# Attention scratch stores: two images per first store, keys by halves of the tokens, weight loads ahead of the stores

## The reference, cut to what matters

```python
def _dilate_attention(q, k, v, head_dim, scale, ksz, dil):      # l0
    ...
    attn = jnp.einsum('bncl,bnckl->bnlk', qr, kp) * scale
    attn = jax.nn.softmax(attn, axis=-1)
    out = jnp.einsum('bnlk,bnckl->bnlc', attn, vp)
```

## Time and profile before

| What | us |
|---|---|
| median of 3 runs | 901.85 |
| profiled execution, its own time | 900.02 |
| its span, first to last instruction | 898.4 |
| TensorE matmuls busy | 668.9 |
| VectorE busy | 403.3 |
| ScalarE busy | 299.2 |
| GpSimd busy | 133.0 |
| TensorE waiting at line 705 for `k_parts` | 35.9 |

### The profile page before, as it was taken

How to read it: one execution, slowest core, us unless ns; L and a number is a source line. 1 busy time by engine, 2 the same in 40 slices (tenths; PEclk the granted TensorE clock), 3 DMA queues, 4 the chain that set the end, 5 groups by cost and what they waited for, 6 DMA issues and landing times. The chain is left out here.

```text
span 898.4 us, 12568 instructions
## 1 busy us (share of the span) xinstructions
PE 668.9 (74%) x3958; PEld 551.4 (61%) x3958; DVE 403.3 (45%) x1010; ACT 299.2 (33%) x594; POOL 133.0 (15%) x185
## 2 busy tenths in 40 slices
PE   5848855998977999519869980299990498698397
PEld 2536634696774999516557770299990267576286
DVE  3647845216255333054648844032311546586501
ACT  2323423223223454113225431044440143245222
POOL 5311110003000000242340003300005306100000
PEclk9988987698988999858879985599996588799689
DMA  3783200533014364113685304347622138751153
GB/s 106 162 222 80 77 19 32 129 101 112 1 39 119 104 178 121 41 53 78 170 248 114 67 7 145 117 109 184 176 67 66 37 80 227 197 124 32 40 131 93
DMA packets 87826, 94.42 MB, mean 105 GB/s; under 512 B 16689, under 2 KB 75972, under 8 KB 87768
## 3 DMA queue, kind: packets, MB, share of 16 engines
q1 hardware_dynamic: 77448, 69.60, 30.3%
q0 software_dynamic: 8656, 23.01, 9.1%
q10 hardware_dynamic: 1680, 1.28, 0.6%
HBM read 68.19 MB, written 25.89 MB: 105 GB/s over the span
## 5 line engine op out<-in xcount | busy, mean ns | idle before, releaser
L816 DVE TENSOR_REDUCE neg_max<-psum 128x4 f32<-128x1024 f32 x72 | 88.0, 1223 | 52.9 <-PE psum L705 52.2
L1610 PE MATMUL psum<-w,area 128*112 128x192 f32 (+1 forms) x576 | 96.2, 326 | 0.0
L1610 PEld LDWEIGHTS psum<-w,area 128*112 128x112 f32 (+1 forms) x576 | 93.4, 183 | 0.0
L705 PE MATMUL psum<-k_parts,q_parts 128*128 128x256 f32 x288 | 57.8, 327 | 46.1 <-DMA k_parts<-k_scratch 35.9
L717 PE MATMUL psum<-q_parts,k_parts 128*128 128x256 f32 x288 | 81.0, 310 | 8.6 <-DVE shift L826 8.6
L705 PEld LDWEIGHTS psum<-k_parts,q_parts 128*128 128x128 f32 x288 | 43.1, 210 | 66.7 <-issue 52.0
L347 PE MATMUL psum<-ident,x_norm 128*96 128x128 f32 x128 | 26.8, 356 | 76.1 <-DVE x_norm L320 76.0
L718 PE MATMUL psum<-shift,ones_r 128*128 128x256 f32 x288 | 77.2, 297 | 0.0
L1871 POOL DMA_INDIRECT area<-result_scratch,f_from_row x32 | 30.8, 963 | 268.2 <-DMA result_scratch<-area 259.0
L717 PEld LDWEIGHTS psum<-q_parts,k_parts 128*128 128x128 f32 x288 | 59.5, 206 | 16.0 <-issue 13.3
L347 PEld LDWEIGHTS psum<-ident,x_norm 128*96 128x96 f32 x128 | 17.4, 161 | 83.2 <-DVE x_norm L320 82.2
(11 more groups left out here) (222 smaller groups left out, 1268.8 us busy)
## 6 DMA issues: line engine op xcount, KB each, us to landing
w<-in_f_w_dram SPq DMA_DIRECT2D x32, 576.0 KB, 4.5
w<-in_f_w_dram SPq DMA_DIRECT2D x16, 384.0 KB, 5.0
w<-in_f_w_dram SPq DMA_DIRECT2D x32, 192.0 KB, 5.4
q_parts<-q_scratch SPq DMA_DIRECT2D x32, 192.0 KB, 3.4
q_scratch<-area POOLq DMA_DIRECT2D x22, 192.0 KB, 4.2
k_parts<-k_scratch SPq DMA_DIRECT2D x63, 64.0 KB, 3.0
q_parts<-q_scratch SPq DMA_DIRECT2D x32, 96.0 KB, 2.8
q_parts<-q_scratch SPq DMA_DIRECT2D x40, 64.0 KB, 2.5
```

The costliest lines, as they stand in the source:

```text
L705: ins = pe.matmul(ps[:, b, IMG_TOK * c:IMG_TOK * (c + 1)], query(2 * s + b, c), k_parts[:, 2 * s + b, :], start=True, stop=True)
L816: ins = dve.tensor_reduce(most, ps[:, 0:2, :].rearrange("p b (c k) -> p (b c) k", c=2), AX_X, ALU.max, negate=True)
L1610: ins = pe.matmul(ps[0:R, 6 + c // 2, D * (c % 2):D * (c % 2 + 1)], x.hidden[:, fc, R * c:R * (c + 1)], net.w2[:, b, fc, :], start=(fc == ...
```

## The change

- SP's first stores hold two images instead of one (`store(..., 0, 2, ...)`), the same number of them.
- A unit of keys is now one half of the channels and one half of the tokens, in the order: first two images of both halves, then the last two. PE computes the key banks in that order, VectorE copies them, ScalarE and VectorE split each as it comes.
- POOL no longer stores image two. It stores images three and four (16 stores in l2 and l3, 8 in l0) and now waits for `scored` to reach 6 before them. One semaphore, `rest_written`, replaces two.
- SP needs no wait for image two, and waits for `rest_written` before image three.
- In l0 `start_loads` of `prep.third` stands ahead of SP's first store instead of behind the last load of image one.

```diff
@@ -481,9 +481,11 @@
     q_parts, k_parts = net.q_parts, net.k_parts
     K0 = 64
     REL = 4
-    units = [(kind, half) for kind in (*range(kinds), KEY) for half in range(2)]
-    first_written = [sem(f"{tag}_first_written{n}") for n in range(len(units))]
-    rest_written = [sem(f"{tag}_rest_written{n}") for n in range(2)]
+    units = [(kind, half, 0, IMGS) for kind in range(kinds) for half in range(2)]
+    of_keys = len(units)
+    units += [(KEY, half, 2 * tc, 2 * tc + 2) for tc in range(2) for half in range(2)]
+    first_written = [sem(f"{tag}_first_written{n}") for n in range(of_keys + 2)]
+    rest_written = sem(tag + "_rest_written")
     query, rel_h, rel_w = (v.rearrange("p h t -> p (h t)").rearrange("p (n a b) -> p n a b", a=SIDE, b=SIDE)
                            for v in (parts.query, *parts.rel_values))
 
@@ -511,14 +513,17 @@
                           src[:, first - HALF_HEADS * half:last - HALF_HEADS * half, :]).then_inc(loaded[piece], DMA)
 
     def take_high(act, first, last):
-        for kind, half in units[first:last]:
-            act.copy(parts.high[kind][half], parts.values[kind][half]).then_inc(high_sb, 1)
+        for kind, half, i, end in units[first:last]:
+            at = slice(IMG_TOK * i, IMG_TOK * end)
+            act.copy(parts.high[kind][half][:, at], parts.values[kind][half][:, at]).then_inc(high_sb, 1)
 
     def take_low(dve, first, last):
         for n in range(first, last):
-            kind, half = units[n]
+            kind, half, i, end = units[n]
+            at = slice(IMG_TOK * i, IMG_TOK * end)
             dve.wait_ge(high_sb, n + 1)
-            dve.tensor_tensor(parts.low[kind][half], parts.values[kind][half], parts.high[kind][half], ALU.subtract).then_inc(low_sb, 1)
+            dve.tensor_tensor(parts.low[kind][half][:, at], parts.values[kind][half][:, at], parts.high[kind][half][:, at],
+                              ALU.subtract).then_inc(low_sb, 1)
 
     def project_tensor(pe):
         if not m.local:
@@ -549,7 +554,7 @@
         for b in range(4):
             if not m.local:
                 pe.wait_ge(rel_h_sb, b + 1)
-            channels(1, b // 2, b % 2, 4 + b)
+            channels(1, b % 2, b // 2, 4 + b)
         if m.local:
             pe.wait_ge(q_sb, 4)
         else:
@@ -587,17 +592,16 @@
             act.wait_ge(low_sb, 2)
             act.wait_ge(rel_w_sb, 4)
             take_high(act, 4, 6)
-        for half in range(2):
-            act.wait_ge(k_sb, 2 * half + 2)
-            take_high(act, 2 * kinds + half, 2 * kinds + half + 1)
+        for b in range(4):
+            act.wait_ge(k_sb, b + 1)
+            take_high(act, of_keys + b, of_keys + b + 1)
 
     def project_vector(dve):
-        def keys(half):
-            for tc in range(2):
-                b = 2 * half + tc
-                dve.wait_ge(qk_ps, 4 + b + 1)
-                dve.tensor_scalar(parts.keys[:, half, 512 * tc:512 * (tc + 1)], ps[0:HC, 4 + b, :],
-                                  m.bq[:, 1, half:half + 1], 0.25, ALU.add, ALU.mult).then_inc(k_sb, 1)
+        def keys(b):
+            half, tc = b % 2, b // 2
+            dve.wait_ge(qk_ps, 4 + b + 1)
+            dve.tensor_scalar(parts.keys[:, half, 512 * tc:512 * (tc + 1)], ps[0:HC, 4 + b, :],
+                              m.bq[:, 1, half:half + 1], 0.25, ALU.add, ALU.mult).then_inc(k_sb, 1)
 
         def values(first):
             for b in (first, first + 1):
@@ -624,10 +628,13 @@
                     take_low(dve, 2 + b, 3 + b)
             take_low(dve, 4, 6)
         keys(0)
-        take_low(dve, 2 * kinds, 2 * kinds + 1)
+        take_low(dve, of_keys, of_keys + 1)
         keys(1)
+        take_low(dve, of_keys + 1, of_keys + 2)
+        for b in (2, 3):
+            keys(b)
         values(0)
-        take_low(dve, 2 * kinds + 1, 2 * kinds + 2)
+        take_low(dve, of_keys + 2, of_keys + 4)
         values(2)
 
     def group(g):
@@ -653,12 +660,19 @@
             def store_first(n):
                 for part, ready in ((0, high_sb), (1, low_sb)):
                     sp.wait_ge(ready, n + 1)
-                    store(sp, *units[n], part, 0, 1, first_written[n])
+                    store(sp, *units[n][0:2], part, 0, 2, first_written[n])
 
             def written(n):
                 sp.wait_ge(first_written[n], 2 * DMA)
 
-            of_keys = 2 * kinds
+            def load_image(i):
+                for piece, (first, last) in enumerate(PIECES):
+                    sp.wait_ge(scored, i * HEADS + (last - HEADS))
+                    load_queries(sp, i, piece)
+                    load_keys(sp, i, piece)
+
+            if prep:
+                start_loads(net, sp, prep.third, prep.loaded)
             for n in range(of_keys):
                 store_first(n)
             for half in range(2):
@@ -667,23 +681,11 @@
                 for piece in (2 * half, 2 * half + 1):
                     load_queries(sp, 0, piece)
                 store_first(of_keys + half)
-                if half == 1:
-
-                    written(of_keys + half)
-                    for piece in (2, 3):
-                        load_keys(sp, 0, piece)
-            if prep:
-                start_loads(net, sp, prep.third, prep.loaded)
-
-            def load_image(i):
-                for piece, (first, last) in enumerate(PIECES):
-                    sp.wait_ge(scored, i * HEADS + (last - HEADS))
-                    load_queries(sp, i, piece)
-                    load_keys(sp, i, piece)
-
-            sp.wait_ge(rest_written[0], DMA * 2 * len(units))
+            written(of_keys + 1)
+            for piece in (2, 3):
+                load_keys(sp, 0, piece)
             load_image(1)
-            sp.wait_ge(rest_written[1], DMA * 2 * len(units))
+            sp.wait_ge(rest_written, DMA * 2 * (of_keys + 2))
             with sp.Fori(2, IMGS) as i:
                 load_image(i)
 
@@ -797,7 +799,7 @@
                     take_mix(i * GROUPS + (s // 2 - 1))
 
             project_scalar(act)
-            act.wait_ge(first_written[2 * kinds], 2 * DMA)
+            act.wait_ge(first_written[of_keys], 2 * DMA)
             for piece in range(2):
                 load_keys(act, 0, piece)
             for _ in all_steps(act, step):
@@ -924,10 +926,12 @@
             pool.wait_ge(v_sb, 4)
             pool.wait_ge(high_sb, len(units))
             pool.wait_ge(low_sb, len(units))
-            for n, (first, last) in enumerate(((1, 2), (2, IMGS))):
-                for kind, half in units:
+
+            pool.wait_ge(scored, HALF_HEADS)
+            for kind in (*range(kinds), KEY):
+                for half in range(2):
                     for part in range(2):
-                        store(pool, kind, half, part, first, last, rest_written[n])
+                        store(pool, kind, half, part, 2, IMGS, rest_written)
             for _ in all_steps(pool, last_step):
                 pass
             if m.local:
```

## The result

| | us |
|---|---|
| changed kernel, median of 20 runs | 896.65 (892.33 to 900.03) |
| kernel before, median of 20 runs | 900.73 (895.85 to 904.73) |
| ratio | 0.9949, interval 0.9934 to 0.9964 |
| span of the profiled execution, before and after | 898.4 and 892.8 |

The change makes the kernel 0.5% faster. 885.6 was forecast, with 876 to 894: the sign is right, the size is a quarter of it, 4.1 us where 16.2 were forecast. (The forecast was added to a median over three runs, 901.85; over twenty it is 900.73, which takes 1.1 us off the distance.) The waits over the whole span show it first: engine, line, waited for, us in total, times, longest.

A forecast was written before the change was run, and what follows sets the result against it. The prediction took TensorE's waits for key parts at the step from image one to two as the bound. Its terms gave -5.8 us in l0 and -5.2 each in l2 and l3, together -16.2, hence 885.6 us, range 876 to 894.

The forecast's parts named there:

- What bounds it: Attention blocks: 29.5 of TensorE's 35.9 us of key-part waits lie at the step from image one to two.
- Part 1: l0: weight loads ahead of the first store make query loads 8 us late (1.3 to 12.4); 13.33 and 0.99 come back.
- Part 2: First stores of two images: first look 1.5 us later in l2 and l3 (0 to 3.6), 0.5 in l0.
- Part 3: Keys by halves of the tokens: nothing charged, between -1.2 and +0.6 us.
- Part 4: l2, l3: POOL's stores after six scored heads leave 3 us stall at image two's third piece; 8.1 and 1.58 come back.
- The sum: Change per block: l0 -5.8, l2 -5.2, l3 -5.2 us, together -16.2 us.
- (c): l0's stall only carried to its start, l0 gaining 1.4 us, 6 us of stall in l2 and l3: 896; chance 0.12.
- (a): l2, l3: DMA engines serve SP's and POOL's queues alike, so the 3 us stalls fall away: 879.6 us; chance 0.20.
- (b): l0: weight loads hide in SP's idle time, first look 1.3 + 0.5 us late instead of 8.5: 878.9; chance 0.15.
- (d): Slower: POOL's round beside image two's loads starves SP's queue longer in l2 and l3: 906.4 us; chance 0.06.

The follow-up runs named there:

- e2: Changed kernel with l0's thirty weight loads moved behind all of SP's image loads; 883.25 us, ratio 0.9815.
- e3: Changed kernel without POOL's wait for six scored heads before its stores of images three and four; 893.29 us, ratio 0.9924.
- e4: Changed kernel with POOL's constants for k_parts and q_parts in l0 issued only once the queries' high parts are there; 896.53 us, ratio 0.9958.
- e5: Kernel before with only the thirty weight loads moved ahead of l0's first store; 905.62 us, ratio 1.0050.
- e8: Kernel before with only the thirty weight loads moved behind all of SP's image loads; 887.36 us, ratio 0.9855.
- e12: Kernel before with only keys by halves of the tokens, first stores still of one image; 902.25 us, ratio 1.0012.
- e1: Changed kernel with l0's thirty weight loads put back behind image one's last key loads, ahead of image two's; 895.17 us, ratio 0.9942.
- e6: Changed kernel with the weight loads last on SP and without POOL's wait for six scored heads; 874.25 us, ratio 0.9714.
- e7: Changed kernel with the weight loads last on SP and POOL's wait moved from 6 scored heads to 18; 906.50 us, ratio 1.0054.
- e10: Changed kernel with 14 of the thirty weight loads ahead of l0's first store and 16 behind all image loads; 886.56 us, ratio 0.9833.
- e9: Changed kernel with the weight loads last and all stores on SP, POOL storing nothing; 874.31 us, ratio 0.9722.

## Why the prediction was wrong

- **What bounds it.** Right: the steps from image one to two, by SP's queue in l0 and by POOL's rounds in l2 and l3 (e2, e3).
- **Part 1, the term that failed most.** 8 + 0.5 us was taken, 13.7 us measured. The step was "20 us of work starts near 18 and ends near 38. The first stores must land before the query loads". To go by the data in the engines and not by the issues was right (e4), but the account was short twice. It had 20 us of work where the trace has 23.3, because it left out the stores' own 0.79 MB, which have to land too. The weight loads' own share was right: in e2, where they run beside little else, queue q1 holds the engines for 67.1% of 95 to 114 us, 12.7 us, and 12.3 were taken. And it let the engines be full from 18 to the end, where they are at 31% from 16 to 20, at 72% from 20 to 24 and at 86% from 32 to 36. So the query loads start at 44.13 and not at 38.5. That the issues ended as late as 38.94 is not what counts: in e4 they ended at 30.68 and the query loads started at 44.62. My upper end was 12.4. Its other half held: 14.3 us should come back, and from the first look to image three l0 needs 13.9 us less.
- **Part 2.** 1.5 us was taken; its size is not shown. The profiled pair has 0.9 and 1.2 us, but the kernels that keep stores of one image (before, e5, e8, e12) have their first looks of l2 and l3 at 38.45 to 41.16, on average 39.5, and those with stores of two images (changed, e1 to e4, e6, e7, e10) at 39.34 to 40.61, on average 39.9. So 0.4 us is the best estimate, within a scatter of over 1 us. The median landing of SP's stores in l2's quiet stretch went from 1.8 us to 2.1 us (418 to 434, changed kernel). By the fit in the Trainium skill ("DMA: Bandwidth & Descriptors", Anatomy of one DMA) the term would have been some 0.4; these traces don't contradict it and are too scattered to confirm it.
- **Part 3.** Right as far as e12 can tell: nothing.
- **Part 4, the second that failed.** 3 us of stall in each of l2 and l3 was taken. From the first look to image three the changed l2 needs 37.63 us, and 31.13 with no round beside it (e9); in l3 36.69 and 31.04. So the round costs 6.5 and 5.7 us. The place, the third piece, was right. "Landed only 8.1 us after its last issue" became 10.2 us (463.33 to 473.52): six issues stood in a queue that has 7% of the engines, where I had added 1 us; POOL began at 455.24 and not at 453.7; and the wait is long enough for TensorE's slow steps again, which I did not add (the four matmuls of the look at 473.52 take 1.22 us and not 0.74).
- **The sum** was -5.8, -5.2 and -5.2; the profiled pair has -0.2, -2.0 and -2.5. These, too, are single executions. Over the four kernels with POOL's two rounds (before, e5, e8, e12) image three of l2 and l3 is at 77.72 to 80.17, on average 79.1, over the five that wait for six heads (changed, e1, e2, e4, e10) at 76.65 to 78.39, on average 77.4: 1.7 us a block, and with l0's 0.2 it makes 3.6 of the medians' 4.1 us.
- **The rivals.** (c), 896 with a chance of 0.12, is what happened: l0's stall carried to its start, and 3 us more than forecast lost to POOL's round in each of l2 and l3. (a) had the queues take equal turns: the 94.3% against 6.9% refute it for this traffic. (b) is refuted by the first look at 53.55, and by e4, whose issues were short and saved nothing. (d), slower, did not come, but two of its kind did: e5, where POOL's rounds met the query loads behind the weight data, and e7, by a copy queued behind a round.

## What to carry to other kernels

An idle queue is not free room: before moving transfers into it, add up the data of all queues in that stretch, and ask who waits for the first landing behind them. Loads that nobody waits for belong behind the last load somebody waits for; that edit of two lines alone (e8) gave three times what the whole change gave. And when a block of stores has to go somewhere, look at both neighbours: whose loads run beside it, and which short instruction stands behind it on its own queue.

## What the runs showed that I had not expected

With POOL's stores of 2 KB rows and SP's loads of 1 KB rows both queued, the engines gave SP's queue 6.9% and 8.2% of their time in two executions, and not a share by halves. In l0 of the changed kernel the first fourteen issues of weight loads took 0.28 to 0.50 us each and those between 21 and 34 mostly 1.4 to 2.5 us. With POOL's constants later (e4) none took over 1.3 us, and the kernel was no faster.
